# Layer boundaries of a four-layer kernel on one core: the scan's last steps in another order, value products moved between shared-expert tiles, the latent space computed among the first attention queries

## The reference, cut to what matters

```python
# layer 1: state-space scan; its feed-forward ends in a layer norm
y = jnp.swapaxes(ys, 0, 1) + x * W_D
y = y * jax.nn.silu(skip)
s = resid + y @ W_out.T
y = shared_out + moe_out
ffn = (y - mu) * jax.lax.rsqrt(var + EPS) * ln_gamma + ln_beta
# layer 2: attention with one shared key/value head; 16 routed experts, capacity 128, and a shared one
v = hidden_states @ Wv.T
shared = jax.nn.silu(x @ sw_gate) * (x @ sw_up) @ sw_down
# layer 3: attention over a latent of 64 features, 16 heads; then a 4-bit feed-forward
latent = x @ W_kv_down
kv = (latent @ W_kv_up).reshape(B, S, N_HEADS, D_HEAD).transpose(0, 2, 1, 3)
scores = jnp.einsum('bhqd,bhkd->bhqk', q, kv) * scale
out = jnp.einsum('bhqk,bhkd->bhqd', jax.nn.softmax(scores, axis=-1), kv)
s = out.reshape(B, S, N_HEADS * D_HEAD) @ W_o
```

## Time and profile before

| | us |
|---|---|
| median of 3 runs (997.34 to 1005.48) | 1002.12 |
| the profiled execution, its own time | 1003.62 |
| its span, first to last instruction | 1001.6 |
| mean granted PE clock over the span | 0.988 |
| PE busy | 940.3 (94%) |
| DVE busy | 686.9 (69%) |

### The profile page before, as it was taken

How to read it: one execution, slowest core, us unless ns; L and a number is a source line. 1 busy time by engine, 2 the same in 40 slices (tenths; PEclk the granted TensorE clock), 3 DMA queues, 4 the chain that set the end, 5 groups by cost and what they waited for, 6 DMA issues and landing times. The chain is left out here.

```text
span 1001.6 us, 13643 instructions
## 1 busy us (share of the span) xinstructions
PE 940.3 (94%) x4684; PEld 564.3 (56%) x4684; DVE 686.9 (69%) x1095; ACT 477.9 (48%) x1007; POOL 288.4 (29%) x254
## 2 busy tenths in 40 slices
PE   6999999989999999999998999988899999999997
PEld 3555564365666566556465555565565556555554
DVE  2989877279999999775635565563866755666653
ACT  3732233798887888233145454553755540111112
POOL 0000020008888888423013232100644440000000
PEclk9999999999999999998999999998999999999999
DMA  4122123040000000019254454302000001111101
GB/s 134 44 80 91 50 71 123 1 123 20 29 22 22 22 22 1 1 41 271 76 151 110 96 108 92 65 1 43 1 2 2 1 2 57 38 32 31 31 1 42
DMA packets 58304, 53.89 MB, mean 54 GB/s; under 512 B 14216, under 2 KB 53225, under 8 KB 58241
## 3 DMA queue, kind: packets, MB, share of 16 engines
q1 hardware_dynamic: 52704, 47.05, 16.0%
q0 software_dynamic: 3072, 4.20, 2.7%
q10 hardware_dynamic: 2464, 1.84, 0.6%
HBM read 44.45 MB, written 5.47 MB: 50 GB/s over the span
## 5 line engine op out<-in xcount | busy, mean ns | idle before, releaser
L1126 POOL TENSOR_TENSOR seen<-state,c_row 128x512 f32<-128x512 f32 x128 | 160.5, 1276 | 102.0 <-DVE state L1146 74.6
L1146 DVE TENSOR_TENSOR_SCAN state<-decay,banks 128x512 f32<-128x512 f32 x128 | 155.3, 1217 | 14.8 <-issue 7.3
L2622 PE MATMUL banks<-xnT,weight 128*128 128x512 f32 x256 | 115.2, 593 | 0.0
L1084 ACT ACTIVATE weighed_x<-dx_tok,b_tok 128x512 f32<-128x512 f32 x124 | 87.6, 709 | 25.7 <-PE banks L1256 24.4
L2318 POOL TENSOR_TENSOR prob<-prob,inverse 128x512 f32<-128x512 f32 x64 | 65.2, 1039 | 106.0 <-DVE inverse L2414 106.0
L1094 ACT ACTIVATE decay<-delta_pairs,A 128x510 f32<-128x510 f32 x128 | 90.4, 706 | 6.2 <-DVE state L1146 6.2
L1256 PEld LDWEIGHTS banks<-ident,weighed_x 128*128 128x128 f32 x512 | 58.6, 140 | 59.2 <-ACT weighed_x L1084 33.3
L2628 ACT ACTIVATE w_WqT<-banks 128x512 f32<-128x512 f32 x32 | 19.1, 597 | 149.2 <-PE banks L2622 149.2
L1256 PE MATMUL banks<-ident,weighed_x 128*128 128x128 f32 x512 | 80.1, 279 | 2.3 <-DVE state L1146 2.3
L2622 PEld LDWEIGHTS banks<-xnT,weight 128*128 128x128 f32 x256 | 48.6, 190 | 48.3 <-issue 46.7
L1270 PE MATMUL banks<-seen,fold 128*64 128x512 f32 x256 | 69.7, 617 | 0.0
(11 more groups left out here) (394 smaller groups left out, 1721.3 us busy)
## 6 DMA issues: line engine op xcount, KB each, us to landing
prob_row<-probs_dram SPq DMA_DIRECT2D x8, 512.0 KB, 3.7
c_row<-c_dram SPq DMA_DIRECT2D x32, 128.0 KB, 2.9
slot_wide_w<-in_L_ffn_w_gate SPq DMA_DIRECT2D x16, 176.0 KB, 2.5
slot_wide_w<-in_L_ffn_w_up SPq DMA_DIRECT2D x16, 176.0 KB, 2.9
slot_down_w<-in_L_ffn_w_down SPq DMA_DIRECT2D x16, 176.0 KB
gate_up_w<-in_L_ffn_gate_up_w SPq DMA_DIRECT2D x8, 256.0 KB, 2.9
delta_pairs<-conv_in SPq DMA_DIRECT2D x8, 256.0 KB, 3.5
w_WqT<-in_L_attn_W_q SPq DMA_DIRECT2D x1, 2048.0 KB, 13.2
```

The costliest lines, as they stand in the source:

```text
L1084: nc.scalar.activation(weighed[:, v % 2, tile, :, j, :], dx_tok[:, 4 * p + tile, :].rearrange("p (g e) -> p g e", g=groups), ACT.Identity, ...
L1126: nc.gpsimd.tensor_tensor(seen[:, u % ring, :], state[:, u % ring, :], c_row[:, v % 4, :], ALU.mult).then_inc(seen_ready, 1)
L1146: nc.vector.tensor_tensor_scan(state[:, u % ring, :], decay[:, u % ring, :, :].rearrange("p b t -> p (b t)"), banks[:, 4 + u % 2, :], 0.0, ...
L2622: last = self.nc.tensor.matmul(self.banks[:, pair + j, :], self.weights.weight[:, s, j, k, tile * P:(tile + 1) * P], self.xnT[:, k, self.c ...
```

## The change: what it does, and the diff

1. **Scan's tail.** The eight statistics of `y` are taken two by two: three pairs inside the scan loop, one unit after `add_lowered`, the last pair in the tail. On DVE the mean, variance and one gate product come ahead of the other three gates. On PE the last `lower` goes ahead of the last two `total`s; the three fillers go; the `W_out` products of the first four tiles go to banks 4 and 5 and no longer wait for the second pass's gates; nine fillers become four. `gamma`, `mix` and `finish` get another order.
2. **Routing.** The values leave the job list: after each of the first four shared jobs, PE makes the values of two tiles in a free part of bank 0; ACT copies them after the fifth shared job. Their two fillers go. DVE's shared products begin after the third one-hot and stand between the one-hots.
3. **Folding.** Two of the four folded banks are made in the norm stage of layer 3, in place of two of its three fillers.
4. **Latent space.** `latent_prepare_stage` and its barrier go. Its products stand among the first four queries; the table of the exponential is loaded by a small activation at the block's start; `lat_tok` is copied after the exponentials of u = 1, and SP waits for it.
5. **Unpacking of the first weights.** Now five parts: 1 (only L2583) in the norm stage, 2 and 3 at the head of the attention block, 4 (one product, three scalings) at pair 4 of batch 1. The buffers lie in memory that is free by then. The later rounds do the same work in the same order.

```diff
@@ scan_stage, DVE @@
+                def measure(b):
+                    dve.wait_ge(y_ready, b + 1)
+                    for t in range(2 * b, 2 * b + 2):
+                        steps.add(nc.vector.bn_stats(stats[:, t, :], y[:, t, :]))
...
                     if r == 0 and b:
                         add_lowered(b - 1)
+                    if r == 1 and b:
+                        measure(b - 1)
                 add_lowered(BATCH - 1)
-                for mi in range(MI):
-                    gate(1, mi)
...
+                measure(BATCH - 1)
...
+                gate(1, 0)
                 dve.wait_ge(std_ready, 1)
...
+                for mi in range(1, MI):
+                    gate(1, mi)
@@ scan_stage, PE @@
+                lower(jobs - 1)
                 total(units - 2)
                 total(units - 1)
-                lower(jobs - 1)
                 pe.wait_ge(scanned, units)
-                keep_busy(nc, banks[:, 4, :], ident, 3)
-                pe.wait_ge(gated_ready, passes * MI)
+                pe.wait_ge(gated_ready, MI)
                 for t in range(NT):
+                    if t == NT // 2:
+                        pe.wait_ge(gated_ready, passes * MI)
...
-                keep_busy(nc, banks[:, 4, :], ident, 9)
+                keep_busy(nc, banks[:, 6, :], ident, 4)
@@ route_stage, PE @@
+                    if first_shared <= n < first_shared + NT // 2:
+                        values(n - first_shared)
+
+                def values(pair_of_tiles):
+                    for t in (2 * pair_of_tiles, 2 * pair_of_tiles + 1):
+                        for k in range(KD):
+                            last = nc.tensor.matmul(banks[:, 0, v_first + t * HEAD2:v_first + (t + 1) * HEAD2],
+                                                    xnT[:, k, t * P:(t + 1) * P], w["Wv"][:, k, :],
+                                                    start=(k == 0), stop=(k == KD - 1))
+                    last.then_inc(values_done, 1)
@@ route_stage, DVE @@
-                    if before + t < len(jobs):
-                        job(before + t)
-                for n in range(before + NT, len(jobs)):
-                    job(n)
+                    if t >= 2:
+                        job(first_shared + t - 2)
@@ work_on_weights @@
     def tensor(pe):
-        keep_busy(nc, banks[:, 3, :], ident, 3)
+        for b in range(FOLDED_EARLY3, UNITS3 // 2):
+            fold_output_weights(nc, w, banks[:, FOLD_BANKS3[b], :], b).then_inc(folded, 1)
+        keep_busy(nc, banks[:, 3, :], ident, 1)
@@ latent_attention_stage @@
+                sp.wait_ge(tokens_ready, 1)
...
+                    if u < 2:
+                        pe.wait_ge(latT_ready, 1)
...
-                for u in range(ahead_q):
-                    query(u)
-                    if u < ahead_s:
-                        score(u)
+                query(0)
+                latent(0)
+                query(1)
+                score(0)
+                latent(1)
+                query(2)
+                score(1)
+                query(3)
+                latent_tokens()
...
+                    if place(u) == (1, 4):
+                        weights.unpack(dve, scratch, 0, 0, 4)
...
+                nc.scalar.activation(exp_table[:, :], xnT[:, 0, 0:1], ACT.Exp)
                 for u in range(ahead_q - 1):
                     query(u)
+                    if u < 2:
+                        act.wait_ge(lat_done, u + 1)
+                        nc.scalar.activation(latT[:, cols[u]], banks[:, 4 + u, :], ACT.Identity).then_inc(latT_ready, 1)
```

More of the change, by code:

```diff
@@ L1387, in route_stage @@
     halves = range(2)
-    jobs = ([("k", 0, 0)] + [("q", g, half) for g in range(2) for half in halves] + [("v", 0, 0)]
+    jobs = ([("k", 0, 0)] + [("q", g, half) for g in range(2) for half in halves]
             + [("s", i, half) for i in range(tiles) for half in halves])
@@ L2432, in keep_mixed @@
                     nc.vector.tensor_copy(s_of(b), banks[:, mix_bank, :]).then_inc(s_ready, 1)
+                for part in (2, 3):
+                    weights.unpack(dve, scratch, 0, 0, part)
                 for u in range(ahead_s):
```

136 lines of the change are left out of this document (64 added, 72 removed).

## The result

The changed kernel takes 985.78 us (median of 9 runs, 983.79 to 991.93) where the kernel before took 999.11 in the same measurement (9 runs, 996.98 to 1005.48): a ratio of 0.988, 95% interval 0.9849 to 0.9911. The forecast was 984.5. A second measurement of the same two kernels gave 0.9873 (0.9834 to 0.9912).

What follows compares the result with a forecast made beforehand. PE bounds it, busy 94% of the span, partly at low clock. Tail 3.2, routing 5.0, folding 1.4, unpacking 1.0 - 0.5 and latent space 8.5 sum to 18.6 us: 1003.6 becomes 985.0, forecast 984.5 against the runs' median; range 979.5 to 992.

Steps and rivals of the forecast that it cites:

- The lower bound, 979.7: Whole kernel: the time if every part ends at its good end, 22.4 us gained in all.
- Term (a): Scan's tail, DVE: `lower` stands behind two `total`s in place of four, 1.4 us earlier.
- Term (b): Scan's tail, DVE: six of eight statistics leave the tail, gaining 2.0 us.
- Term (c): Scan's tail, DVE: gates and `gamma`s fill idle time inside the tail, gaining 1.8 us, bounds 0 and 2.0.
- Term (d): Scan loop, DVE: the six statistics moved there cost 0.3 us, bounds 0 and 2.0.
- Term (e): Layer 2's norm stage: PE stands 3.8 us before it, and a clock fall costs 1.7 us, bounds 0 and 3.4.
- The loss to the clock: Routing, PE: spreading the values among shared jobs keeps the clock up, so all 3.4 us lost there are gained.
- Rival 1: Tail and latent stretch: the clock takes back more, 1.7 + 2.4 us, giving 989; chance 0.16.
- Rival 2: Scan loop and batch 1: moved statistics and last unpacking are uncovered on DVE, 1.7 + 2.35 us more, 989; chance 0.09.
- Rival 3: Layer 3 attention: the first `weigh` waits for SP's token-row transfers, 8 us go back, 993 to 997; chance 0.06.
- Rival 4: Routing: values between shared jobs hold the clock at 1.2 GHz, 1009, or 1024 if lowering too; chance 0.03.
- the allowance of 1.0 for a fall: Latent stretch of layer 3: a clock fall there costs 1.0 us, bounds 0 and 3.4, cutting 9.5 to 8.5.

Runs made afterwards that it cites:

- stats_late: The changed kernel with all eight statistics of `y` in the tail, none in the scan loop: 991.16 us, ratio 0.9892 to the kernel before.
- pieces: The changed kernel with part 4 of the unpacking cut in four pieces, behind the inverses of pairs 2 to 5: 990.78 us, ratio 0.991 to the kernel before.
- latent_first: The changed kernel with all latent products and their evictions ahead of the queries, still in the attention block: 989.99 us, ratio 0.9914 to the kernel before.
- combined: The changed kernel with part 4 of the unpacking in four pieces, beta additions on VectorE and six fillers behind the output product: 983.39 us, ratio 0.9826 to before.
- betas_dve: The changed kernel with the four additions of beta done by VectorE instead of GpSimd: 985.05 us, ratio 0.9861 to the kernel before.
- after_again: The changed kernel once more, with no edit, for a second trace and more runs: 988.82 us.
- d_only: The kernel before with only the latent space, five-part unpacking and earlier table load changed, folding as before: 994.19 us, ratio 0.9915.
- fill8: The changed kernel with eight fillers instead of four behind the scan's output product: 989.94 us, ratio 0.989 to the kernel before.
- b_only: The kernel before with only the routing stage's move of the values: 1001.48 us, ratio 0.9995.

## Why the prediction was right, and where it was not

**The time.** 985.78 against 984.5. Part of the hit is luck: two errors cancel. The sum was 18.6 us, taken from one profiled execution at 1003.6; the medians differ by 13.3, and at equal clock the change is worth 13.1. That execution had a mean clock of 0.988, below the 0.9905 of the runs of before, so its low stretches entered the sum as if the change removed them. The base, 984.5 + 18.6 = 1003.1, was 4.0 us above the measured 999.11. So 5.3 us too much gain and 4.0 us too much base leave the miss of 1.3. "1.5 us above the median of the runs" rested on three runs, and only 0.5 of the 1.5 was taken off; the 69 runs of before in the later measurements have a median of 1000.9. The lower bound, 979.7, is counted from 1002.1, another base than the forecast's.

**Tail.** DVE sets the boundary, PE stands ahead of it: right (3.8 us foretold, 4.32 measured). Predicted 5.2 less 0.3, measured 5.2 less 0.7. Term (a), 1.4: `add_lowered` came 1.72 us earlier behind the last scan (7.10 to 5.38). Term (b), 2.0: 1.84. Term (c), 1.8: the rest, 1.6. Term (d), 0.3, was under-sized: 0.70 (`stats_late`). The `add_lowered` row alone did not bound it; how the loop comes by the 0.7 us was not followed further. Term (e), 1.7 us for the fall: in the norm stage 0.8 to 0.9 in five of the eight traces that have one (8.38 without it), 1.4 and 1.8 in two, and 2.2 where PE stood longest. Four of the eight (`pieces`, `latent_first`, `stats_late`, `combined`) then have a second fall right behind the norm stage, and the 12.23 us from the router products to the place products become 13.9: 1.7 us more.

**The rule on fillers.** Over the fourteen traces, PE stood 1.26 to 1.35 us ahead of layer 2's norm in five, and the clock was 1.00 in the norm stage of all five. It stood 2.03 to 6.16 us in nine, and the clock fell in eight of them (not in `betas_dve`, 3.74 us). So at this boundary the traces agree with the rule of the Trainium skill (TensorE: Matmul & The Clock Gate, What's actually happening) that activity releases the throttle. They do not agree with it as the whole account: 0.50 was granted for 20.5 us (`after_again`) and 10.2 us (`d_only`, 452.7 to 462.9) to a PE that was busy throughout. In the changed kernel's two traces the fall at the boundary costs 0.8 and 0.9 us, and `fill8` shows that paying for it in fillers returns nothing measurable.

**Routing.** The stage did what was foretold (5.0 against 5.1; last product 1.49 us behind PE, foretold 1.7), and the step that failed is the one on the clock: "The loss to the clock, 10.60 - 7.2 = 3.4 us, goes if the clock stays up", and then "I take all of it". That it leaves this stretch is right in nine of nine traces. That the program is rid of it is wrong in four of the nine, which have a fall in the experts: `b_only` loses 3.0 us to it, `after_again` 8.8. The runs of `b_only` have a mean clock of 0.9880, no higher than the 0.9901 of the runs of before beside them. The durable part is the fillers' 1.75 us. Rival 1 (the clock takes back more) named the right thing with a wrong reason, since it tied the loss to waits and fillers at the two boundaries: these falls come with PE fully busy.

**Folding and unpacking.** 1.4 foretold, 1.5 measured; 1.0 foretold, 0.9 measured. Part 4 was sized at 0.5 by the 0.81 us that DVE waits per pair; it was 1.3. The lead of the scores, into which the prediction let part of the 2.85 fall, is no cover for the exponentials: they wait for DVE's flips two pairs behind. They start 5.30 us apart at the block (718.03 to 723.33) instead of 3.42, so the wait hid 1.0 us of the 2.8; the next two pairs follow after 2.91 us each and make up a part, and at the second `weigh` 1.3 us are lost. Cut in pieces of 0.67 to 0.94 us it costs nothing.

**Latent space.** 16.2 us foretold to the first exponential, 16.25 measured; the allowance of 1.0 for a fall was not needed. Of the 9.45 us 2.7 are order (`latent_first`). The 6.75 left were not parted by a run of their own. An estimate from `d_only`: its stages are 9.2 us shorter (9.45 + 1.06 in the norm stage - 1.27 in batch 1), of which 4.7 are left at equal clock; so 4.5 are clock and some 2.2 the block boundary and the earlier table load. The four traces with the old block all have a clock of about 0.8 in it (25.56 to 27.27 us long), the ten with the new block none below 1.00. By its row, 25.70 x 0.20, the trace of before spent 5.1 us of clock there, not all of it on the path. So these falls do belong to their place, a stretch full of waits, and the change did remove them. That the mean clock is no higher afterwards (0.9903) fits with falls at two places where before has none: in layer 2's norm stage, in eight of the nine traces in which PE stands 2 us or more ahead of it, and in the last batch (784 to 801 us), in six of the ten with the new block and none of the four with the old.

**Rivals 2 to 4.** Rival 2 (the moved DVE work is not covered) in part: 0.4 and 0.8 us over the terms instead of 4.05. Rival 3 (the first `weigh` waits): no, 20.98 us from the exponential to the first `weigh`, before 20.86. Rival 4 (the values hold the clock down): none of the nine traces with the values spread has a low clock among the shared jobs.

**Open.** What calls a fall while PE is fully busy (488.6 to 509.1 us in one trace, 508 to 515 in another) was not found. Most of these stretches have heavy transfers (DMA share 0.94 to 0.97), but so has the stretch ahead of the values at clock 1.00 (0.88), and the longest has 0.04. It was not tried to take the transfers away. Ahead of the four falls in the experts PE had stood 1.0 to 1.5 us within the last 4 to 5 us (1.11 of 5.30 in `b_only`), but traces without such a fall have the same waits at the same places, and ahead of the fall among the values of before PE was busy without a gap (4.40 of 4.40 us).

## What to carry to other kernels

Before a low-clock stretch of one trace is booked as a gain, look at a second execution or at a kernel that shares the code: what PE's work costs at full clock is the durable part, and a line of time against mean clock over the runs shows 1 to 2 us where medians hide 5. That line does not tell what the change does to the clock: for this, compare the mean clocks themselves. Put long side work of an engine in a tight ring of waits in pieces no longer than its idle time per round; in one block it is paid for. Where VectorE ends a stage, look at what GpSimd does beside it before reordering VectorE.

## What the runs showed of the hardware that was not expected

The granted clock stood at half for 20.5 us with PE busy all the time, in one of two executions of the same program (mean 0.56 over 23.50 us, PE busy 23.15 of them); it cost 8.8 us, more than any part of the change but one brings. And two engines' elementwise operations on SBUF operands are not parallel in this tail: GpSimd's four additions of 1.66 us cost VectorE 3.0 us (2.84 - 1.28, 1.16 - 0.67, 1.64 - 0.69), so that doing them on VectorE at 0.64 us each was faster than giving them away.
